# Preparing quantised weights on four engines: VectorE's rounding passes move to ScalarE, scales to GpSimd, context clipping to ScalarE, and the inverse transform ahead of a weight chunk

## The chip, the cores and the metric

The kernel runs on one core of one Trainium2 chip. The metric is the device time of one execution in microseconds (us). Three executions of the kernel before took 1344.51, 1345.06 and 1346.99 us; the median is 1345.06 us.

## The reference, cut to what matters

A two-layer decoder over 2 x 256 tokens of width 512. Layer 0 is an autocorrelation block, an 8-bit product of the tokens with a context, and a feed-forward block with block-quantised weights. Layer 1 is attention over a cache, attention over the context, and a mixture of eight experts. The part that the change touches is in layer 0:

```python
def _quant_elem(x, mbits):           # mbits = 1 for weights
    e = jnp.maximum(jnp.floor(jnp.log2(jnp.maximum(jnp.abs(x), 2.0 ** (-30)))), 0.0)
    step = jnp.exp2(e - mbits)
    return jnp.clip(jnp.round(x / step) * step, -max_norm, max_norm)
def _mx_quant(x, mbits):             # blocks of 32 along the last dimension
    scale = jnp.exp2(jnp.floor(jnp.log2(amax)) - EMAX)
    return (_quant_elem(xb / scale, mbits) * scale).reshape(s)
...
q = jnp.clip(jnp.round(ctx / s + z), 0, 255)      # context, 8 bits
...
corr = irfft(f * conj(f)); weights, delay = top_k(corr, 6)   # autocorrelation taps
x = x + sum_k softmax(weights)[k] * roll(x, delay[k])
```

## The kernel before, in words

Every engine runs a program of its own, written out by hand: it executes its instructions in order, and waits on named semaphores. Nothing reorders them, so the order of the code on an engine is the order of its work.

While VectorE, GpSimd and ScalarE do layer 0's small blocks, the feed-forward weights are brought in as 15 chunks, 11 of 128x1024 (gate and up) and 4 of 128x1408 (down), numbered c = 0 to 14 (`CHUNKS`). SyncE loads chunk c into one of two buffers (`WX`, `load_chunk`). VectorE finds the largest magnitude of each block of 32 (line 916), makes a power-of-two scale and its reciprocal from it (918, 919, 921 or 923), multiplies the chunk by the reciprocal, takes each element's exponent by a mask (936 or 961), makes the rounding constant from it (939 or 962), adds it (940 or 963), subtracts it (943 or 965), clips to +-6 (944 or 966), and multiplies the scale back (945). TensorE then transposes the chunk (`weight_step`, L1325), and ScalarE copies it out of PSUM (L630, L636). For chunks 0 to 5 VectorE does all of it (`weight_chunk`). From chunk 6 on (`SHARED`) GpSimd does the two products with the scales (`normalised`, L521, and `scaled`, L528).

Among the chunks stand other jobs. VectorE finds each row's six taps after chunk 2 (L1005 to L1018), and finishes the taps' softmax after chunk 3 (L1022 to L1024), for which ScalarE computes an exponential (L661). GpSimd fetches the tapped rows by 20 indirect DMAs (L513), and quantises the context, which arrives in four pieces through one buffer `CN` (L502, L505, L507; SyncE loads the next piece once the third of these is done, semaphore `cn_used`). TensorE projects the context for the later attention in 16 steps (`context_step`, L1304 for keys, L1307 for values), two behind each chunk of the table `CONTEXT_AT`; ScalarE copies each step out of PSUM (L624), and there are two PSUM banks for them. The inverse transform (L1345 to L1347) and the weighted sum of the taps (`taps`, L1356, placed by `TAPS_AT`) are TensorE's too. After the last chunk VectorE adds the taps' result to the tokens (L1035), and the second layer norm follows. The rest, attention above all, comes after it.

## Time and profile before

| | |
|---|---|
| Median of three runs | 1345.06 us |
| The profiled execution: its time, its span | 1347.69 us, 1345.8 us |
| Busy over the span: TensorE, VectorE | 1163.9 us (86%), 901.7 us (67%) |
| Busy over the span: ScalarE, GpSimd | 555.8 us (41%), 538.7 us (40%) |
| Weight stage on VectorE | from 23.25 us to 184.45 us |
| VectorE busy from 23.20 to 184.50 us | 152.0 us of 161.3 |

An engine with a large busy share bounds the program only where the others wait for it. So the averages over the whole span say little here: the stage before 184.45 us and the attention after 237 us are bounded by different engines. Instruction rows give the start and the duration; brackets behind a row give the idle time ahead of it and who ended it. PE is TensorE, DVE is VectorE, ACT is ScalarE, POOL is GpSimd, SPq is SyncE's DMA queue.

### The profile page before, as it was taken

The page shows a single profiled execution, that of the slowest core. Times are in us where ns is not written, and L with a number is a line of the kernel's source. Part 1 is how long each engine was busy: PE and PEld are TensorE (multiplying, and loading weights), DVE is VectorE, ACT ScalarE, POOL GpSimd, SP SyncE. Part 2 cuts the span into 40 slices and gives each one's busy share as a digit, 9 for nine tenths or more (in the row PEclk, how much of TensorE's full clock was granted, in tenths as well). Part 3 has the DMA queues.
Part 4 walks back from the last instruction along what each step waited for, and adds up shares of the span by engine and source line. Part 5 has one row for each costly group of instructions (what it writes and reads, how often), then busy time and mean ns, then how long its engine had stood idle before and what let it go on. Part 6 is the DMA issues. An engine that isn't in the chain of part 4 may idle for free.

```text
span 1345.8 us, 16908 instructions
## 1 busy us (share of the span) xinstructions
PE 1163.9 (86%) x5655; PEld 880.9 (65%) x5660; DVE 901.7 (67%) x1432; ACT 555.8 (41%) x1094; POOL 538.7 (40%) x372
## 2 busy tenths in 40 slices
PE   4939624759899999999999999879899999987999
PEld 2413311336688888888888887745678788875787
DVE  6999998886486868686868686554354545543543
ACT  1211222222565656565656565522454535442111
POOL 3774520010464646464645454410454545441000
PEclk9968955879999999999999999989799999999899
DMA  7172442001101010101010101230001010001122
GB/s 289 63 234 91 151 173 74 20 32 40 44 17 59 17 58 16 58 16 58 16 58 16 51 0 55 56 121 24 7 12 37 12 29 0 1 24 63 46 95 78
DMA packets 38834, 77.70 MB, mean 58 GB/s; under 512 B 11395, under 2 KB 19588, under 8 KB 35588
## 3 DMA queue, kind: packets, MB, share of 16 engines
q1 hardware_dynamic: 37188, 71.86, 16.4%
q0 software_dynamic: 1600, 5.24, 1.2%
q8 instruction: 27, 0.44, 0.1%
q14 instruction: 19, 0.16, 0.0%
HBM read 69.75 MB, written 9.44 MB: 59 GB/s over the span
## 4 chain that ended last, share of the span: by engine, by line
PE 71%; DVE 18%; issue 5%; ACT 3%; DMA 1%; POOL 1%; SPq 1%; POOLq 0%; DVEq 0%; ACTq 0%
PE PS L1441 15%; PE PS L1439 15%; PE PS L1440 15%; PE PS L1505 9%; PE PS L1479 5%; DVE nmax L1114 2%; PE PS L1356 2%; PE PS L1407 1%; PE PS L1610 1%; DVE blkamax L916 1%; PE PS L1304 1%; DMA cs<-in_freqs 1%; PE PS L1579 1%; PE PS L1307 1%; DVE PTL L1162 1%
## 5 line engine op out<-in xcount | busy, mean ns | idle before, releaser
L555 POOL TENSOR_TENSOR arena<-arena,rsum 128x768 f32<-128x768 f32 x192 | 281.8, 1468 | 471.5 <-DVE rsum L1119 471.5
L1114 DVE TENSOR_REDUCE nmax<-PS 128x1 f32<-128x768 f32 x192 | 183.5, 956 | 215.8 <-PE PS L1441 213.9
L739 ACT ACTIVATE arena<-PS,nmax 128x768 f32<-128x768 f32 x192 | 173.3, 903 | 252.9 <-DVE nmax L1114 252.8
L1505 PE MATMUL PS<-identf,arena 128*128 128x128 f32 x1152 | 161.1, 276 | 27.7 <-DVE PTL L1162 15.1
L1505 PEld LDWEIGHTS PS<-identf,arena 128*128 128x128 f32 x1152 | 135.6, 141 | 63.8 <-issue 38.8
L1162 DVE TENSOR_TENSOR PTL<-PS,PTH 128x384 fp32r<-128x384 f32 x256 | 129.6, 547 | 1.7 <-ACT PTH L755 1.1
L755 ACT ACTIVATE PTH<-PS 128x384 fp32r<-128x384 f32 x256 | 111.7, 488 | 40.0 <-PE PS L1505 37.7
L1479 PE MATMUL PS<-arena 128*96 128x256 f32 x384 | 87.9, 380 | 0.0
L542 POOL TENSOR_TENSOR WQL<-arena,WQH 128x512 fp32r<-128x512 f32 (+1 forms) x48 | 58.5, 1220 | 60.9 <-ACT WQH L615 60.9
L1439 PE MATMUL PS<-WOH,OTH 128*128 128x512 f32 (+1 forms) x192 | 75.8, 395 | 4.1 <-DVE OTL L1135 3.0
L1439 PE MATMUL PS<-HTH,WQH 128*128 128x512 f32 (+1 forms) x192 | 77.0, 401 | 0.0
L1441 PE MATMUL PS<-WOH,OTL 128*128 128x512 f32 (+1 forms) x192 | 76.3, 397 | 0.0
L1440 PE MATMUL PS<-HTL,WQH 128*128 128x512 f32 (+1 forms) x192 | 76.3, 397 | 0.0
L1441 PE MATMUL PS<-HTH,WQL 128*128 128x512 f32 (+1 forms) x192 | 76.1, 396 | 0.0
L1440 PE MATMUL PS<-WOL,OTH 128*128 128x512 f32 (+1 forms) x192 | 75.7, 394 | 0.0
L1441 PE MATMUL PS<-PTH,VSL 128*128 128x512 f32 x192 | 75.6, 394 | 0.0
L1440 PE MATMUL PS<-PTL,VSH 128*128 128x512 f32 x192 | 75.5, 393 | 0.0
L1129 DVE TENSOR_TENSOR QTL<-arena,QTH 128x512 fp32r<-128x512 f32 (+1 forms) x40 | 67.7, 1694 | 10.6 <-ACT QTH L731 10.6
L1439 PE MATMUL PS<-PTH,VSH 128*128 128x512 f32 x192 | 74.7, 389 | 0.0
L1479 PEld LDWEIGHTS PS<-arena 128*96 128x96 f32 x384 | 61.7, 164 | 17.7
L542 POOL TENSOR_TENSOR WOL<-arena,WOH 128x512 fp32r<-128x512 f32 (+1 forms) x48 | 70.7, 1474 | 0.0
L1119 DVE RECIPROCAL rsum<-psum_exp 128x1 f32<-128x1 f32 x192 | 31.5, 164 | 52.5 <-ACT arena L739 38.7
(243 smaller groups left out, 2528.6 us busy)
## 6 DMA issues: line engine op xcount, KB each, us to landing
arena<-in_wq SPq DMA_DIRECT2D x32, 256.0 KB, 2.6
arena<-in_wo SPq DMA_DIRECT2D x8, 1024.0 KB, 4.8
arena<-in_expert_w SPq DMA_DIRECT2D x8, 1024.0 KB, 4.8
arena<-in_wgu SPq DMA_DIRECT2D x11, 512.0 KB, 3.7
arena<-v_dram SPq DMA_DIRECT2D x8, 384.0 KB, 3.5
arena<-in_wq SPq DMA_DIRECT2D x16, 192.0 KB, 2.8
arena<-in_wo SPq DMA_DIRECT2D x4, 768.0 KB, 5.9
arena<-in_wd SPq DMA_DIRECT2D x4, 704.0 KB, 4.0
```

Of the source, the lines that this page charges most:

```text
L542: pool.tensor_tensor(fr(lo), raw, hi, ALU.subtract).then_inc(s["w_ready"], 1)
L555: pool.tensor_tensor(PR[:, u % 4, :], PR[:, u % 4, :], rsum[:, u % 4:u % 4 + 1].broadcast_to([P, KEYS]), ALU.mult).then_inc(s["pn_ready"], 1)
L739: act.activation(PR[:, slot, :], SC[pair][:, 0:KEYS], ACT.Exp, bias=nmax[:, slot:slot + 1], accum_out=psum_exp[:, slot:slot + 1]).then_inc ...
L755: act.activation(fr(PTH[:, (u // 4) % 2, 3 * half:3 * half + 3, u % 4 * P:(u % 4 + 1) * P]), bank(B_PT[half])[:, 0:3 * P].rearrange("p (k ...
L1114: dve.tensor_reduce(nmax[:, slot:slot + 1], SC[pair][:, 0:KEYS], AX.X, ALU.max, negate=True)\
L1129: dve.tensor_tensor(fr(QTL[0:hd, j, :]), QT[0:hd, j, :], QTH[0:hd, j, :], ALU.subtract)\
L1162: dve.tensor_tensor(fr(PTL[:, (u // 4) % 2, ks, cols]), bank(B_PT[half])[:, 0:3 * P].rearrange("p (k c) -> p k c", k=3), PTH[:, (u // 4) % ...
L1439: pe.matmul(out, fr(xh), fr(yh), start=start, stop=False)
L1440: pe.matmul(out, fr(xh), fr(yl), start=False, stop=False)
L1441: return pe.matmul(out, fr(xl), fr(yh), start=False, stop=stop)
L1479: mm = pe.matmul(bank(B_OT)[0:hd, b * S:(b + 1) * S], VS2[:, b, k, :], PT[:, j % 2, k, b * S:(b + 1) * S], start=k == 0, stop=k == KK - 1)
L1505: mm = pe.transpose(bank(B_PT[half])[:, k * P:(k + 1) * P], PR[:, u % 4, c * P:(c + 1) * P], identf[:])
```

## The change

On VectorE a chunk is now two halves, `weight_normalised(c)` (maxima, scales, product with the reciprocal, exponent mask) and `weight_rounded(c)` (two fused operations, clip), and the order is a pipeline: normalised(c + 1) stands ahead of rounded(c). The rounding constant `max(m, 1) * ROUND/2` becomes a ScalarE activation `magic(c)`, Relu(ROUND/2 * m - ROUND/2), in bf16; the missing ROUND/2 is added inside the two `scalar_tensor_tensor` operations. GpSimd does the product with the scale for all 15 chunks, and no product with the reciprocal. In the context's quantisation the clip moves from GpSimd to three ScalarE activations, and GpSimd's last operation takes its constants from SBUF (`qconst`) instead of from the instruction. GpSimd's 20 gathers no longer stand together but in fours ahead of `scaled(3)` to `scaled(7)`. On TensorE the inverse transform stands ahead of weight chunk 1, the context steps 2 to 7 one chunk later, and the taps behind chunks 9 to 12. SyncE loads chunks 6 and 7 ahead of the second half of the transposed context.

```diff
-        SHARED = 6
-        CONTEXT_AT = {0: (0, 1), 1: (2, 3), 2: (4, 5), 3: (6, 7), 5: (8, 9), 6: (10, 11), 7: (12, 13), 8: (14, 15)}
-        TAPS_AT = {5: 0, 6: 1, 8: 2, 9: 3}
+        CONTEXT_AT = {0: (0, 1), 2: (2, 3), 3: (4, 5), 4: (6, 7), 5: (8, 9), 6: (10, 11), 7: (12, 13), 8: (14, 15)}
+        TAPS_AT = {9: 0, 10: 1, 11: 2, 12: 3}
...
-            load_chunk(5)
+            for c in range(5, 8):
+                load_chunk(c)
             sp.wait_ge(s["ectx_psum"], 8)
             sp.dma_start(CTXT, ctx_t[1].rearrange("(k p) t -> p k t", p=P)).then_inc(s["ctxt_in"], 16)
-            for c in range(6, len(CHUNKS)):
+            for c in range(8, len(CHUNKS)):
...
+            def context_quantised(n):
                 pool.wait_ge(s["ctxn_in"], 16 * (n + 1))
                 pool.tensor_scalar(CN, CN, inv_s[:, 1:2], qs[:, 3:4], ALU.mult, ALU.add)\
+                    .then_inc(s["cn_scaled"], 1)
+                pool.wait_ge(s["cn_clipped"], n + 1)
+                pool.tensor_scalar(CQ[:, n // 2, (n % 2) * 2:(n % 2) * 2 + 2, :], CN, qconst[:, 0:1], qconst[:, 1:2],
+                                   ALU.mult, ALU.add).then_inc(s["cn_used"], 1)
...
+            context_quantised(0)
+            context_quantised(1)
+            for c in range(3):
                 scaled(c)
+                if c < 2:
+                    context_quantised(c + 2)
...
+            for c in range(3, len(CHUNKS)):
+                for n in range(4 * (c - 3), min(4 * (c - 2), RT * LAGS)):
+                    gather(n)
+                scaled(c)
...
+            def magic(c):
+                act.wait_ge(s["wexp_ready"], c + 1)
+                if c >= 2:
+                    act.wait_ge(s["wq_rounded"], c - 1)
+                act.activation(weight_magic(c), WM[:, 0:CHUNKS[c]], ACT.Relu, bias=neg_magic[:, 0:1],
+                               scale=ROUND / 2).then_inc(s["magic_ready"], 1)
...
+            for c in range(len(CHUNKS)):
+                if c + 2 < len(CHUNKS) and c != 2:
+                    magic(c + 2)
+                for w in [c] if c < NCH else [2 * c - NCH, 2 * c - NCH + 1]:
+                    weight_step(w)
+                for n in CONTEXT_AT.get(c, ()):
+                    context_step(n)
+                if c < 2:
+                    context_clipped(c + 2)
+                if c + 1 in TAPS_AT:
+                    tap_diagonals(TAPS_AT[c + 1])
+                if c == 2:
                     act.wait_ge(s["tap_diff"], 1)
                     act.activation(tapw[:], tapv[:], ACT.Exp).then_inc(s["tap_exp"], 1)
+                    magic(c + 2)
...
+            def weight_normalised(c):
...
+                block_scale(w, n, 0.25, blkinvs[c % 3], blkscales[c % 3])
+                dve.tensor_tensor(blocks(nn, n), blocks(w, n), spread(blkinvs[c % 3], n // MX), ALU.mult)\
+                   .then_inc(s["wx_used"], 1)
+                dve.wait_ge(s["wx_used"], c + 1)
+                if c:
+                    dve.wait_ge(s["magic_ready"], c)
+                dve.tensor_scalar(WM[:, 0:n].bitcast(U32), nn.bitcast(U32), EXPONENT, None, ALU.bitwise_and)\
+                   .then_inc(s["wexp_ready"], 1)
+            def weight_rounded(c):
...
+                dve.wait_ge(s["magic_ready"], c + 1)
+                step(dve.scalar_tensor_tensor(nn, mm, ROUND / 2, nn, ALU.add, ALU.subtract))
                 if c >= 2:
                     dve.wait_ge(s["wt_psum"], c - 1 if c - 2 < NCH else NCH + 2 * (c - 2 - NCH) + 2)
+                step(dve.scalar_tensor_tensor(q, mm, ROUND / 2, nn, ALU.add, ALU.subtract))
                 dve.tensor_scalar(q, q, 6.0, -6.0, ALU.min, ALU.max).then_inc(s["wq_rounded"], 1)
...
+            weight_normalised(3)
+            weight_rounded(2)
...
+            weight_normalised(4)
+            weight_rounded(3)
             dve.wait_ge(s["tap_exp"], 1)
```

VectorE, one chunk in the middle of the stage before: the five passes of a 128x1024 chunk, then the next chunk's block maxima and scales (`arena` is the large work area in which most buffers lie, `HT` the second buffer for the normalised chunk).

```order
L961 TENSOR_SCALAR arena<-HT 128x1024
L962 TENSOR_SCALAR arena<-arena 128x1024
L963 TENSOR_TENSOR HT<-HT,arena 128x1024
L965 TENSOR_TENSOR arena<-HT,arena 128x1024
L966 TENSOR_SCALAR arena<-arena 128x1024
L916 TENSOR_REDUCE blkamax<-arena 128x32
L918 TENSOR_SCALAR blkamax<-blkamax 128x32
L919 TENSOR_SCALAR blkscale<-blkamax 128x32
```

The same engine and place now: maxima and scales, product and mask of one chunk, then the three passes of the chunk ahead of it.

```order
L952 TENSOR_REDUCE blkamax<-arena 128x32
L954 TENSOR_SCALAR blkamax<-blkamax 128x32
L955 TENSOR_SCALAR blkscale<-blkamax 128x32
L956 RECIPROCAL blkinv<-blkscale 128x32
L966 TENSOR_TENSOR arena<-arena,blkinv 128x1024
L971 TENSOR_SCALAR arena<-arena 128x1024
L979 SCALAR_TENSOR_TENSOR arena<-arena 128x1024
L982 SCALAR_TENSOR_TENSOR arena<-arena 128x1024
L983 TENSOR_SCALAR arena<-arena 128x1024
```

The pass L962 has left VectorE, and the product L966 has come back to it.

ScalarE before, from the copy of context step 0 to the exponential of the taps (L661), which stands behind context steps 4 and 5 (128x384).

```order
L624 ACTIVATE arena<-PS 96x512 x2
L630 ACTIVATE arena<-PS 128x4x256
L624 ACTIVATE arena<-PS 96x512 x2
L630 ACTIVATE arena<-PS 128x4x256
L624 ACTIVATE arena<-PS 128x384 x2
L661 ACTIVATE tapw<-tapv 128x24
```

ScalarE now, from the clip of context piece 2 (L673 to L677) to the exponential (L701).

```order
L673 ACTIVATE arena<-arena,qconst 128x1024
L675 ACTIVATE arena<-arena,qconst 128x1024
L677 ACTIVATE arena<-arena,qconst 128x1024
L666 ACTIVATE arena<-arena,neg_magic 128x1024
L638 ACTIVATE arena<-PS 128x4x256
L673 ACTIVATE arena<-arena,qconst 128x1024
L675 ACTIVATE arena<-arena,qconst 128x1024
L677 ACTIVATE arena<-arena,qconst 128x1024
L638 ACTIVATE arena<-PS 128x4x256
L632 ACTIVATE arena<-PS 96x512 x2
L701 ACTIVATE tapw<-tapv 128x24
L666 ACTIVATE arena<-arena,neg_magic 128x1024 x2
```

Two clips of the context and the copies of the weight chunks 1 and 2 and of the context steps 2 and 3 now stand between the copy of context step 1 and the exponential.

## Rows read from the trace of the kernel before

**Rows 1.** Busy time by stage, with TensorE's granted clock, DMA share and GB/s

```profile
23.20:67.80 44.60, 42.11 (x127) 19.56 (x125) 42.56 (x73) 8.48 (x13) 28.46 (x10) 1.00 0.27 93
67.80:96.00 28.20, 8.99 (x35) 5.41 (x36) 26.41 (x37) 3.25 (x5) 22.01 (x19) 0.62 0.74 239
96.00:184.50 88.50, 56.84 (x192) 27.58 (x190) 83.03 (x82) 21.26 (x44) 42.16 (x19) 0.81 0.37 120
```

**Rows 2.** Timeline of VectorE, the first half of the stage (start, duration)

```profile
23.25 1.22 DVE L916 TENSOR_REDUCE blkamax<-arena 128x32 f32<-128x1024 f32 x1
...
44.20 1.29 DVE L999 TENSOR_TENSOR arena<-arena 128x512 f32<-128x512 f32 x2
...
56.46 0.42 DVE L1005 COPY arena<-PS 128x256 f32<-128x256 f32 x1
...
67.79 1.21 DVE L916 TENSOR_REDUCE blkamax<-arena 128x32 f32<-128x1024 f32 x1
...
71.12 0.69 DVE L936 TENSOR_SCALAR arena<-arena 128x1024 uint32<-128x1024 uint32 x1
...
72.69 1.23 DVE L940 TENSOR_TENSOR arena<-arena 128x1024 f32<-128x1024 f32 x1
...
75.67 1.23 DVE L945 TENSOR_TENSOR arena<-arena,blkscale 128x1024 bf16<-128x1024 bf16 x1
...
77.33 1.21 DVE L916 TENSOR_REDUCE blkamax<-arena 128x32 f32<-128x1024 f32 x1
```

**Rows 3.** Timeline of VectorE, a 128x1408 chunk and the stage's end

```profile
165.45 1.61 DVE L916 TENSOR_REDUCE blkamax<-arena 128x44 f32<-128x1408 f32 x1
167.10 1.12 DVE L918 TENSOR_SCALAR blkamax<-blkamax 128x44 uint32<-128x44 uint32 x1
...
168.82 0.83 DVE L961 TENSOR_SCALAR arena<-HT 128x1408 uint32<-128x1408 uint32 x1
169.68 3.12 DVE L962 TENSOR_SCALAR arena<-arena 128x1408 f32<-128x1408 f32 x1
...
184.45 2.47 DVE L1035 TENSOR_TENSOR X<-X,PS 128x512 f32<-128x512 f32 x4
```

**Rows 4.** Timeline of VectorE, a fused operation in the feed-forward block

```profile
240.34 1.62 DVE L1080 SCALAR_TENSOR_TENSOR arena<-arena,PS 128x1408 f32<-128x1408 f32 x1
```

**Rows 5.** Timeline of GpSimd: context piece 2 and 3, gathers, a product with scales

```profile
50.40 3.96 POOL L507 TENSOR_SCALAR arena<-arena 128x1024 bf16<-128x1024 f32 x1
58.15 1.20 POOL L502 TENSOR_SCALAR arena<-arena,inv_s,qs 128x1024 f32<-128x1024 f32 x1 [3.79 <-DMA arena<-in_ctx]
...
68.50 1.23 POOL L513 DMA_INDIRECT arena<-h,tapoff  x1 [1.72 <-DVE tapoff L1014]
...
96.78 0.95 POOL L513 DMA_INDIRECT arena<-h,tapoff  x1 [0.30 <-issue]
...
106.69 1.91 POOL L528 TENSOR_TENSOR arena<-arena,blkscale 128x1024 bf16<-128x1024 bf16 x1 [3.61 <-DVE arena L966]
```

**Rows 6.** Groups of instructions on ScalarE up to 236 us (busy, mean ns)

```profile
L610 ACT ACTIVATE H<-X,neg_mean 128x512 f32<-128x512 f32 x12 | 7.7, 710 | 15.0 <-DVE neg_mean L879 15.0
L700 ACT ACTIVATE KCH<-arena 128x1024 fp32r<-128x1024 f32 x4 | 3.9, 1046 | 0.0
```

**Rows 7.** Timeline of TensorE: pairs of context steps, a sum of taps

```profile
38.48 7.06 PE L1304 MATMUL PS<-arena 128*96 128x512 f32 x16
...
77.78 7.26 PE L1307 MATMUL PS<-arena 128*128 128x384 f32 x16
...
132.38 5.38 PE L1307 MATMUL PS<-arena 128*128 128x384 f32 x16
...
141.07 4.56 PE L1356 MATMUL PS<-arena 128*128 128x512 f32 x10 [2.86 <-ACT arena L650]
```

**Rows 8.** Timeline of SyncE's DMA queue behind the taps

```profile
162.25 24.04 SPq L381 DMA_DIRECT2D arena<-in_kcache  x16
...
212.63 1.77 SPq L398 DMA_DIRECT2D arena<-in_wq  x4
```

More of the change, by code:

```diff
@@ L482, in _ @@
             pool.memset(minus_half[:], -0.5).then_inc(s["consts"], 1)
+            pool.memset(neg_magic[:], -ROUND / 2).then_inc(s["consts"], 1)
+            for i, v in enumerate((1.0, -128.0, ROUND, ROUND + 255.0, 255.0)):
+                pool.memset(qconst[:, i:i + 1], v).then_inc(s["consts"], 1)
             pool.wait_ge(s["pool_chain"], 2)
@@ L651, in tap_diagonals, with context_clipped @@
                        .then_inc(s["dg_ready"], 1)
-            squared(0)
-            transposed(0)
+            def magic(c):
+                act.wait_ge(s["wexp_ready"], c + 1)
+                if c >= 2:
+                    act.wait_ge(s["wq_rounded"], c - 1)
+                act.activation(weight_magic(c), WM[:, 0:CHUNKS[c]], ACT.Relu, bias=neg_magic[:, 0:1],
+                               scale=ROUND / 2).then_inc(s["magic_ready"], 1)
+            squared(0)
+            def context_clipped(n):
+                act.wait_ge(s["cn_scaled"], n + 1)
+                act.activation(CN, CN, ACT.Identity, bias=qconst[:, 2:3]).then_inc(s["act_chain"], 1)
+                act.wait_ge(s["act_chain"], 2 * n + 1)
+                act.activation(CN, CN, ACT.Relu, bias=qconst[:, 3:4], scale=-1.0).then_inc(s["act_chain"], 1)
+                act.wait_ge(s["act_chain"], 2 * n + 2)
+                act.activation(CN, CN, ACT.Relu, bias=qconst[:, 4:5], scale=-1.0).then_inc(s["cn_clipped"], 1)
+            transposed(0)
+            act.wait_ge(s["consts"], 8)
+            context_clipped(0)
+            magic(0)
+            magic(1)
+            context_clipped(1)
             for m in range(KT):
@@ L910, in transposed, with block_scale @@
                            .then_inc(s["ht_lo"], 1)
[L912 removed]
+            def block_scale(src, n, down, blkinv=blkinv, blkscale=blkscale):
                 nb = n // MX
@@ L940, in weight_chunk @@
-                step(dve.tensor_tensor(nn, nn, mm, ALU.add))
+                if c >= 3:
+                    dve.wait_ge(s["wq8_ready"], c - 2)
+                block_scale(w, n, 0.25, blkinvs[c % 3], blkscales[c % 3])
[4 more added lines that the diff above has]
+                    dve.wait_ge(s["magic_ready"], c)
@@ L956, in chunk_rounded @@
-            def chunk_rounded(c):
-                n = CHUNKS[c]
-                nn, mm, q = (WN, WN2)[c % 2][:, 0:n], WM[:, 0:n], WQ8[:, c % 2, 0:n]
-                dve.wait_ge(s["wn_ready"], c - SHARED + 1)
-                step(dve.tensor_scalar(mm.bitcast(U32), nn.bitcast(U32), EXPONENT, None, ALU.bitwise_and))
-                step(dve.tensor_scalar(mm, mm, 1.0, ROUND / 2, ALU.max, ALU.mult))
-                step(dve.tensor_tensor(nn, nn, mm, ALU.add))
-                dve.wait_ge(s["wt_psum"], c - 1 if c - 2 < NCH else NCH + 2 * (c - 2 - NCH) + 2)
-                step(dve.tensor_tensor(q, nn, mm, ALU.subtract))
+                step(dve.scalar_tensor_tensor(q, mm, ROUND / 2, nn, ALU.add, ALU.subtract))
@@ L1025, in _ @@
                .then_inc(s["tapw_ready"], 1)
-            for c in range(4, SHARED):
-                weight_chunk(c)
-            chunk_scales(SHARED)
-            for c in range(SHARED, len(CHUNKS)):
+            for c in range(4, len(CHUNKS)):
                 if c + 1 < len(CHUNKS):
-                    chunk_scales(c + 1)
-                chunk_rounded(c)
+                    weight_normalised(c + 1)
+                weight_rounded(c)
             for r in range(RT):
@@ L1347, in _ @@
                 pe.matmul(o, SQ[0:1, 2, rows], nyq_sb[0:1, :], start=False, stop=True).then_inc(s["corr_psum"], 1)
-            for n in CONTEXT_AT[1]:
-                context_step(n)
+            weight_step(1)
             def taps(r):
```

95 lines of the change are left out of this document (27 added, 68 removed).

## The prediction, made before the changed kernel was run

> **What bounds the kernel now.** I read the busy times by stage first. In the weight stage VectorE is busy for 42.56 of 44.60 us, 26.41 of 28.20 and 83.03 of 88.50, ScalarE for a fifth at most [rows 1]. So up to 184.45 us, where the taps are added, VectorE's own passes set the time; the other engines matter only where they make it wait. Next the timeline of VectorE gives marks: A 23.25 (first chunk), B 67.79 (taps found, chunk 3 begins), C 77.33 (softmax of the taps done, chunk 4 begins), D 184.45 [rows 2, 3]. What follows D keeps its order and its work; it moves as a block if D moves. I count at D alone.
>
> One pass costs more than its elements. The rounding constant L962 takes 3.12 us for 1408 elements, the mask L961 of the same size 0.83; and L918 takes 1.12 us for 44 elements [rows 3]. Each stands where GpSimd is at work on a product with scales: VectorE's single-source passes wait for it, its maxima (1.61 before L918) do not.
>
> **VectorE's new work.** For 128x1024, maxima, scales, product and mask run from 67.79 to 71.12 + 0.69: 4.05 with the gap. Add, subtract and clip run from 72.69 to 75.67 [rows 2]: 2.98; I take 2.9, as two fused operations take their place and no pass waits behind the clip. The trace has no fused operation on two SBUF tensors, one in bf16. The nearest takes 1.62 us for 1408 elements [rows 4], 1.15 ns each, the rate of the 1.23 us for 1024 of L940 [rows 2]; I take that, 1.26 with its gap. The lower end is the same; the upper is a fused operation at two passes' price, 2.5. So a chunk costs 6.95 where it cost 9.0 (77.33 - 67.79 = 9.54, of which 0.5 is the taps' softmax). For 1408: 168.82 - 165.45 = 3.37, less 0.93 of waiting, plus product 1.66 and mask 0.87, with gaps 5.05; rounding 2 x 1.66 + 0.5 = 3.8 [rows 3, 4].
>
> To B: 4 first halves 16.2, 3 second halves 8.7, the power sum 1.2, the taps' search 67.79 - 56.46 = 11.3, and 0.8 of waits behind GpSimd [rows 2]: 23.25 + 38.2 = 61.4, against 67.79.
>
> From C to D: 6 x 4.05 + 4 x 5.05 + 7 x 2.9 + 4 x 3.8 = 80.0. On top come the waits behind `scaled`, which now starts as each chunk's clip ends, just when VectorE begins a maximum. A product of 1.91 [rows 5] outlasts 1.25 by 0.66 (five times), a 1408 maximum by 0.3 (twice), and the long product costs 0.93 (twice): 5.8. In chunks 5 to 7 GpSimd has four gathers too, at (96.78 - 68.50)/19 = 1.49 us each [rows 5]: 5.9 + 1.9 = 7.8 a chunk, against VectorE's 7.6. The product then starts some 0.3 late, three times. Together 7 us, so C to D is 87.0, against 107.1.
>
> **The new wait, at C.** The exponential of the taps' softmax stands behind a long queue on ScalarE. I follow it. The context's first product takes 1.20; GpSimd's last takes 3.96 now with constants in the instruction, and its new form has them in SBUF, as the 1.20 one has [rows 5]. I take 1.2 and keep 3.96 for the range. A ScalarE pass over 1024 elements takes 1.05, and the one with a bias operand, 0.71 for 512, bounds it from above at 1.4 [rows 6]; I take 1.16, so three in a chain are 3.5. Piece 1 is asked for at 27.1, behind the load of chunk 2 that waits for chunk 0's product (23.25 + 3.3); piece 3 took 3.8 to land [rows 5], this one shares the DMA engines with a chunk and gets 4.8: 31.9, 33.2 scaled, 36.8 clipped, 38.0 stored. `scaled(0)` 40.0, transposes and context steps 0 and 1, 7.06 [rows 7]: 47.6. ScalarE copies, then clips piece 2 to 51.7; stored 53.0. Piece 3 needs 3.8 from there to land [rows 5], and 1.2 + 3.5 + 1.2: 62.6. `scaled(2)` 64.5. Context steps 2 and 3: 0.6 + 7.0, and TensorE has idled for 9 us by then. After the idle stretch from 67.80 to 96.00 with its granted clock of 0.62 [rows 1] a pair of value steps took 7.26, at full clock 5.38 [rows 7]; I add 2.1: 74.1. Copy and exponential: 74.9. VectorE would be at the softmax at 61.4 + 6.95 + 1.6 (behind `scaled(2)`) = 69.9, so it stands for 5 us. C comes at 75.5, against 77.33. The same 5 us hide anything lost before B.
>
> D = 75.5 + 87.0 = 162.5, which is **21.9 us earlier**.
>
> **What I cost at nothing.** `magic(c)`, 1.1 us (1.5 for the long chunks), is hidden: it stands behind the copy and two context steps of chunk c - 3, done at least 6 us before VectorE's next mask. In chunks 5 and 6, each with two key steps of 3.5 and a second context tensor that SyncE asks for only at 90.2 by this count, TensorE finishes about when `magic(8)` and `magic(9)` are due; no wait in my count, but 6 us of slack for `magic(9)` at most. Taps: chunk 12 is transposed at 152.7, the sum takes 5.4 [rows 7], ends 158.0; VectorE needs it at 162.5. SyncE's 16 key loads come behind it, 24.04 us, to about 186 with the issue; the load of wq that follows now waits to 212.63, which is D + 28.2 [rows 8], and would be due at 190.7. So 4 us of slack there. GpSimd's six small memsets lie in its idle start.
>
> Against the profiled execution, 1347.69, this gives 1325.8. That execution is 2.6 above the median; from the median, 1345.06 - 21.9 = **1323.2**.
>
> A rule speaks against the change. ScalarE idles in the stage: 21.26 of 88.50 us busy [rows 1], and passes of 1.16 on it are not on the path. The Trainium skill (ScalarE: Activation LUTs, Rules for kernel authors) says to use VectorE, not ScalarE, for Relu, add and multiply. By that rule the constant would stay on VectorE, 11 x 0.72 + 4 x 0.87 = 11.4 us, and the time would be 1334.6. The trace speaks for the engine that is free.
>
> **The rivals.**
> - GpSimd's last context pass stays slow. For it: its output is bf16, as that of the 3.96 row [rows 5]. Against: the only visible difference of the 1.20 row is where its constants lie, besides that type. It delays the exponential to 85.4, and D to 173.0: 1333.7.
> - TensorE holds up ScalarE, hence the constants. The clock was 0.62 and 0.81 in this stage [rows 1], and I assume it full from 75 us on. For full: a chunk's key pair and transposes fill 7.6 us, a value pair 5.9; a key pair after 38 us took 7.06 at clock 1.00 [rows 1, 7]. If each step from 2 on took 1.5 times as long, VectorE would wait 3.2 and 2.3 us for constants: D 169.8, 1330.4. At twice (half clock throughout) the exponential comes at 79.7, then masks 9 to 12 wait 6.0, 6.6, 2.8 and 4.9, and D is 188.3: **1348.9, slower than before**. It crosses at 1.9 times.
> - The taps are late: at half clock each sum takes 10.6, the last ends at 169.4: D 169.5, 1330.1.
> - The change doesn't do what it says: the fused operations are slower than the passes they replace. At 1.8 each for 1024, D is 175.4, 1336.0; at 2.1 nothing is gained; at 2.5, 1357. Against: rows 4's rate.
> - It is better than I count: no idle-clock penalty and products that VectorE doesn't feel give D 153.4: 1314.0. Against: L918's 1.12 [rows 3].
>
> **How the numbers follow.** A difference under 0.2% (2.7 us) can hardly be told from none here. Chances: forecast, within 1316 to 1329, 0.66; slow context pass 0.10; TensorE late in part (1.2 to 1.8 times, or the taps) 0.10; fused operations somewhat slow 0.05; better than 1316, 0.03; about no change 0.02; slower, by the clock 0.02, by the fused operations 0.02. The range 1315 to 1336 holds the forecast and most of the next three. Faster 0.94, same 0.02, slower 0.04.
>
> **What would show it.** Maxima of the 1024 chunks 7.6 to 7.9 us apart on VectorE, where chunk 3 took 9.0; fused operations at 1.23 and 1.62; an idle stretch of about 5 us ahead of the tap sum's reduction, ended by ScalarE's exponential; the small L918-like operation still at 0.8 to 1.2; ScalarE's clips at 1.1 to 1.2; D near 162.5. Wrong would be idle time ahead of the mask or the fused operations, ended by ScalarE, or ahead of D's addition, ended by TensorE.

## The result: 1327.2 us, 18.8 less than before

The changed kernel's four executions took 1326.07 to 1328.56 us, median 1327.2; four of the kernel before on the same chip took 1344.51 to 1349.08, median 1346.03. The ratio is 0.9858, with a 95% interval of 0.9836 to 0.988. The forecast was 1323.2, with a range of 1315 to 1336. Five more executions later gave a median of 1327.43, so the comparisons below are made with 1327.3.

The marks in the profiled execution (1326.17 us, span 1324.3):

| mark | before | predicted | after |
|---|---|---|---|
| A, first chunk | 23.25 | 23.25 | 22.40 |
| B, taps found | 67.79 | 61.4 | 64.39 |
| C, softmax of the taps done | 77.33 | 75.5 | 78.88 |
| D, the taps' addition | 184.45 | 162.5 | 169.90 |
| from D to the end of the span | 1161.35 | the same | 1154.4 |

So the total is right by two errors that happen to cancel: D came 7.4 us later than predicted, and the part behind D, which was to move as a block, was 7.0 us shorter. That they cancel is luck; with the first alone the sum would have come to 1330.6. Of the 14.55 us gained at D, 0.85 are there at A already: a small VectorE operation just ahead of it, which took 1.01 beside GpSimd's slow pass over the context, takes 0.17 now.

Busy time by stage of the changed kernel, to be read as [rows 1] (span of the window; then PE, PEld, DVE, ACT and POOL busy; PEclk, DMA share, GB/s). VectorE still sets the stages before B and behind C, but with 7.0 idle us behind C; between B and C it idles for 5.7 of 14.5. An operation that is held up by another engine while it runs counts as busy here.

```profile
22.40:64.40 42.00, 31.08 (x88) 14.06 (x86) 40.49 (x72) 20.56 (x22) 14.00 (x8) 0.93 0.34 120
64.40:78.90 14.50, 11.18 (x36) 5.12 (x37) 8.78 (x14) 3.00 (x6) 12.41 (x10) 0.72 0.43 134
78.90:169.90 91.00, 69.10 (x231) 33.88 (x229) 83.98 (x94) 36.69 (x60) 36.75 (x23) 0.88 0.44 146
```

Its timeline of VectorE, the places where it stood or was slow, and two that ran as predicted (start, duration; in brackets idle time and who ended it):

```profile
32.19 2.11 DVE L982 SCALAR_TENSOR_TENSOR arena<-arena 128x1024 bf16<-128x1024 bf16 x1
...
39.51 2.92 DVE L979 SCALAR_TENSOR_TENSOR arena<-arena 128x1024 f32<-128x1024 bf16 x1
...
65.86 1.84 DVE L955 TENSOR_SCALAR arena<-blkamax 128x32 f32<-128x32 f32 x1
...
78.35 0.18 DVE L1044 TENSOR_REDUCE tapm<-tapw 128x4 f32<-128x24 f32 x1 [5.41 <-issue]
...
82.81 1.22 DVE L979 SCALAR_TENSOR_TENSOR arena<-arena 128x1024 f32<-128x1024 bf16 x1
...
94.38 1.19 DVE L954 TENSOR_SCALAR blkamax<-blkamax 128x32 uint32<-128x32 uint32 x1
...
105.55 1.22 DVE L952 TENSOR_REDUCE blkamax<-arena 128x32 f32<-128x1024 f32 x1 [4.53 <-DMA arena<-in_wgu]
...
163.91 1.62 DVE L979 SCALAR_TENSOR_TENSOR arena<-arena 128x1408 f32<-128x1408 bf16 x1
165.56 3.86 DVE L982 SCALAR_TENSOR_TENSOR arena<-arena 128x1408 bf16<-128x1408 bf16 x1
...
169.90 2.47 DVE L1054 TENSOR_TENSOR X<-X,PS 128x512 f32<-128x512 f32 x4
```

A fused operation takes 1.22 or 1.62 where nothing is in its way, as forecast. Two waits stand out: 5.41 us ahead of L1044, for which this trace names no releaser (three others, with the same wait, name ScalarE's exponential), and 4.53 us ahead of chunk 8's maxima. GpSimd's timeline, same kernel, shows the other side of the slow passes:

```profile
31.44 1.79 POOL L513 TENSOR_SCALAR arena<-arena,inv_s,qs 128x1024 f32<-128x1024 f32 x1 [6.97 <-DMA arena<-in_ctx]
36.88 2.16 POOL L516 TENSOR_SCALAR arena<-arena,qconst 128x1024 bf16<-128x1024 f32 x1 [3.65 <-ACT arena L677]
39.01 2.34 POOL L530 TENSOR_TENSOR arena<-arena,blkscale 128x1024 bf16<-128x1024 bf16 x1
...
54.74 1.20 POOL L516 TENSOR_SCALAR arena<-arena,qconst 128x1024 bf16<-128x1024 f32 x1 [9.98 <-ACT arena L677]
...
164.07 3.87 POOL L530 TENSOR_TENSOR arena<-arena 128x1408 bf16<-128x1408 bf16 x1 [7.14 <-DVE arena L983]
```

Read the two together at the end. L979 ends at 165.5; GpSimd's product, called at 164.07, takes 2.56 from there (165.5 + 2.56 = 168.1), and shows 3.87. L982, called at 165.56, takes its 1.62 from the end of that product and shows 3.86. By these times each waits for the whole of the other.

ScalarE's and TensorE's timelines show why L1044 stood: the exponential L701 ended at 78.3 (74.9 predicted), behind the context steps 2 and 3, which TensorE worked on from 68.55.

```profile
53.49 1.15 ACT L677 ACTIVATE arena<-arena,qconst 128x1024 f32<-128x1024 f32 x1
...
78.11 0.21 ACT L701 ACTIVATE tapw<-tapv 128x24 f32<-128x24 f32 x1
```

```profile
41.92 8.69 PE L1323 MATMUL PS<-arena 128*96 128x512 f32 x16
...
67.72 1.03 PE L1344 MATMUL PS<-identb,arena 128*128 128x128 bf16 x8 [9.24 <-POOL arena L530]
68.55 9.03 PE L1323 MATMUL PS<-arena 128*96 128x512 f32 x16
```

SyncE's DMA queue, where chunk 8's load stands behind that of the context's second half (which waits for context step 7):

```profile
96.20 0.38 SPq L372 DMA_DIRECT2D arena<-in_ctx_t  x1
96.63 12.63 SPq L346 DMA_DIRECT2D arena<-in_wgu  x3
```

### The profile page after: what moved, and what is told of

Read it like the earlier page. It is cut to its first block, busy times and chain, and to the rows that moved or that the text cites. A ratio compares the mean times of both kernels' runs of the same rounds, so it can differ in the third digit from the quotient of the medians.

```text
span 1324.3 us, 16950 instructions
## 1 busy us (share of the span) xinstructions
PE 1160.2 (88%) x5655; PEld 877.6 (66%) x5660; DVE 882.2 (67%) x1420; ACT 586.1 (44%) x1121; POOL 504.7 (38%) x371
## 4 chain that ended last, share of the span: by engine, by line
PE 68%; DVE 20%; issue 6%; ACT 2%; DMA 2%; POOL 1%; SPq 1%; POOLq 0%; DVEq 0%; ACTq 0%
PE PS L1457 16%; PE PS L1458 16%; PE PS L1459 15%; PE PS L1523 9%; PE PS L1497 5%; DVE nmax L1133 2%; DVE blkamax L952 2%; DVE arena L982 2%; DVE arena L979 1%; PE PS L1628 1%; DVE arena L966 1%; DMA cs<-in_freqs 1%; PE PS L1597 1%; DVE PTL L1181 1%; PE PS L1307 1%
## 5 line engine op out<-in xcount | busy, mean ns | idle before, releaser
L1523 PE MATMUL PS<-identf,arena 128*128 128x128 f32 x1152 | 159.5, 274 | 27.9 <-DVE PTL L1181 15.4
```

Of the source, the lines that this page charges most:

```text
L1523: mm = pe.transpose(bank(B_PT[half])[:, k * P:(k + 1) * P], PR[:, u % 4, c * P:(c + 1) * P], identf[:])
```

## The experiments

All are edits of the changed kernel, unless stated; times are medians of 4 to 5 executions (12 for the last). Medians of the same kernel differ by 2 to 3 us between batches, so smaller differences are read from the marks of the trace alone. The marks vary too: in traces of kernels with the same order ahead of chunk 8, the wait for it took 4.53 to 5.02 us, and D of the changed kernel itself differs by 0.6.

| run | C | D | time | ratio to before, 95% |
|---|---|---|---|---|
| changed kernel | 78.88 | 169.90 | 1327.2 | 0.9858 (0.9836 to 0.9880) |
| changed kernel, again | 78.97 | 170.49 | 1327.43 | 0.9848 (0.9833 to 0.9863) |
| chunk 8 first | 79.2 | 167.78 | 1326.24 | 0.9842 (0.9819 to 0.9864) |
| exponential early | 75.24 | 162.98 | 1321.18 | 0.9810 (0.9787 to 0.9833) |
| constant on VectorE | 79.12 | 174.29 | 1333.93 | 0.9903 (0.9880 to 0.9926) |
| clip on GpSimd | 82.09 | 173.72 | 1330.40 | 0.9868 (0.9843 to 0.9893) |
| inverse transform late | 83.48 | 172.21 | 1329.25 | 0.9870 (0.9852 to 0.9888) |
| additions sooner | 79.05 | moved | 1325.80 | 0.9842 (0.9826 to 0.9858) |
| three moves | 75.14 | moved | 1320.46 | 0.9806 (0.9790 to 0.9822) |
| GpSimd's last constants in the instruction | 78.40 | 169.81 | 1324.42 | 0.9827 (0.9808 to 0.9846) |
| scale on VectorE | 76.40 | 170.77 | 1327.29 | 0.9854 (0.9838 to 0.9871) |
| three moves and those constants | 75.38 | moved | 1320.33 | 0.9795 (0.9779 to 0.9810) |
| kernel before, again | | 184.27 | 1349.38 | 1.0012 (0.9998 to 1.0025) |

### Chunk 8's load ahead of the context's second half

```diff
-            for c in range(5, 8):
+            for c in range(5, 9):
                 load_chunk(c)
             sp.wait_ge(s["ectx_psum"], 8)
             sp.dma_start(CTXT, ctx_t[1].rearrange("(k p) t -> p k t", p=P)).then_inc(s["ctxt_in"], 16)
-            for c in range(8, len(CHUNKS)):
+            for c in range(9, len(CHUNKS)):
```

> Changed kernel with one thing moved on SyncE's queue: the load of weight chunk 8 stands ahead of the second transposed context instead of behind it. Theory: VectorE's 4.5 us of idle time ahead of chunk 8's maxima came only from that order (the load was issued at 96.63, behind a wait for context step 7, and landed after 1 MB of context). Then the idle time is gone, and the taps' addition, mark D, comes at 165.4 instead of 169.90; the whole 4 to 5 us faster than the changed kernel. Rival: the context steps 8 and 9 start later by as much, ScalarE's constants for chunks 8 and 9 become late, and VectorE waits for those: D at 168 or later.

The wait of 4.53 us is gone, so its cause is shown. But D gained only 2.12 of it, and came (167.78) just below where the rival had it. VectorE now ran ahead of the others: the mask of a later chunk stood 0.93 us for ScalarE's constant, as the rival said, and the small operations behind a maximum lost 1.3 us more to GpSimd's product; C was 0.3 later. VectorE's timeline of this run:

```profile
102.47 1.18 DVE L954 TENSOR_SCALAR blkamax<-blkamax 128x32 uint32<-128x32 uint32 x1
...
114.23 0.69 DVE L971 TENSOR_SCALAR arena<-arena 128x1024 uint32<-128x1024 uint32 x1 [0.93 <-ACT arena L666]
```

### The exponential ahead of the copy of chunk 2

```diff
             for c in range(len(CHUNKS)):
                 if c + 2 < len(CHUNKS) and c != 2:
                     magic(c + 2)
+                if c == 2:
+                    act.wait_ge(s["tap_diff"], 1)
+                    act.activation(tapw[:], tapv[:], ACT.Exp).then_inc(s["tap_exp"], 1)
                 for w in [c] if c < NCH else [2 * c - NCH, 2 * c - NCH + 1]:
                     weight_step(w)
+                if c == 2:
+                    magic(c + 2)
                 for n in CONTEXT_AT.get(c, ()):
                     context_step(n)
```

(and the same three lines are taken out behind the context steps.)

> Changed kernel with ScalarE's order changed in one place: the exponential of the taps' softmax stands ahead of the copy of weight chunk 2, and the rounding constant of chunk 4 ahead of the copies of context steps 2 and 3. Theory: the 5.4 us that VectorE stood still at mark C were this exponential's place in the queue; C comes at 73.5 instead of 78.88, and D 5.4 to 7.3 us earlier (the wait for chunk 8's load shrinks too): 162.6 to 164.5. Rival: the wait only moves to the next thing that comes from that chain, the constants or the transposes of chunks 2 to 4, and D stays above 168.

The theory held but for C: the reduction behind the exponential began at 72.88 with no idle time ahead of it, D came at 162.98, 6.92 earlier, and the time fell by 6.1. C came at 75.24, not at 73.5, since a small softmax operation now waits for GpSimd's product (2.02 us); and 0.78 us are left of the wait for chunk 8. It is the one edit whose gain is clear of the spread between batches.

```profile
73.30 2.02 DVE L1047 TENSOR_TENSOR tapw<-tapw,tapm 128x24 f32<-128x24 f32 x1
...
98.20 1.22 DVE L953 TENSOR_REDUCE blkamax<-arena 128x32 f32<-128x1024 f32 x1 [0.78 <-DMA arena<-in_wgu]
...
162.98 2.47 DVE L1055 TENSOR_TENSOR X<-X,PS 128x512 f32<-128x512 f32 x4
```

### The rounding constant back on VectorE

```diff
+                dve.tensor_scalar(weight_magic(c), WM[:, 0:n], 1.0, ROUND / 2, ALU.max, ALU.mult)\
+                   .then_inc(s["magic_ready"], 1)
...
-                step(dve.scalar_tensor_tensor(nn, mm, ROUND / 2, nn, ALU.add, ALU.subtract))
+                step(dve.scalar_tensor_tensor(nn, mm, 0.0, nn, ALU.add, ALU.add))
```

(the second fused operation likewise, the waits ahead of the pass are not shown, and ScalarE's `magic` is left out.)

> Changed kernel with the rounding constant back on VectorE, as one single-source pass with bf16 output (0.7 to 0.9 us for each of the 15 chunks, 11.4 us in all); ScalarE has no part in it. Theory: VectorE bounds the stage except at its waits (5.4 us at C, 4.5 at chunk 8), which swallow what is added ahead of them: of 11.4 us some 2.9 before C and 2.2 before chunk 8 are absorbed, so D at about 176 (6 us later). Rival A: VectorE is not the bound, D stays within 1 us of 169.90. Rival B: the pass pays for GpSimd as well, with every gather and product that it meets, and costs 15 us or more.

The time rose by 6.6 us and D by 4.39; 2.0 more lie in a stretch of attention far behind D, which is looked at in the last experiment. The passes themselves took 8.5 us for eleven and 3.6 for four, 12.1 together. The waits at C (5.41 us, now none) and for chunk 8 (4.53, now 0.84) took most of that off, since VectorE reached those places later. D came 1.7 below the theory's 176; both rivals fell. The prediction had put this version 11.4 us above its forecast: it had the passes about right, and took nothing off for the waits that absorb them.

The Trainium skill (ScalarE: Activation LUTs, Rules for kernel authors) would keep multiply and maximum on VectorE. Followed here, that rule costs 4.4 us at D: VectorE's pass over 128x1024 is the shorter one (0.69 us against ScalarE's 1.15), but it lies on the path, and ScalarE's does not.

### The clip of the context on GpSimd again

```diff
+                pool.tensor_scalar(CN, CN, qconst[:, 0:1], qconst[:, 1:2], ALU.max, ALU.min)\
+                    .then_inc(s["cn_clipped"], 1)
...
-                pool.tensor_scalar(CQ[:, n // 2, (n % 2) * 2:(n % 2) * 2 + 2, :], CN, qconst[:, 0:1], qconst[:, 1:2],
-                                   ALU.mult, ALU.add).then_inc(s["cn_used"], 1)
+                pool.tensor_scalar(CQ[:, n // 2, (n % 2) * 2:(n % 2) * 2 + 2, :], CN, qconst[:, 2:3], qconst[:, 3:4],
+                                   ALU.add, ALU.add).then_inc(s["cn_used"], 1)
```

with 0, 255 and the two rounding constants in `qconst`, and ScalarE's clips left out.

> Changed kernel with the context's clip and rounding back on GpSimd in three passes as before the change, but all constants read from SBUF instead of from the instruction; ScalarE has no clip. Theory: what made two of these passes cost 3.6 to 4.0 us was where their constants were, so each takes 1.2 to 1.3 us, a piece takes 3.7 instead of 5.9, the exponential no longer comes late, C at about 73.5 and D 5 to 7 us earlier than 169.90. Rival: maximum and minimum are slow on GpSimd in themselves (3.6 us): a piece takes 6.1, C and D stay within 1.5 us.

GpSimd's timeline of this run:

```profile
18.39 3.78 POOL L516 TENSOR_SCALAR arena<-arena,qconst 128x1024 f32<-128x1024 f32 x1
22.27 3.83 POOL L518 TENSOR_SCALAR arena<-arena,qconst 128x1024 bf16<-128x1024 f32 x1
...
59.76 1.20 POOL L513 TENSOR_SCALAR arena<-arena,inv_s,qs 128x1024 f32<-128x1024 f32 x1 [1.61 <-DMA arena<-in_ctx]
```

All three have their constants in SBUF. The (max, min) and the (add, add) pass take 3.8 us, the (multiply, add) pass 1.20; before the change the two slow ones, with their constants in the instruction, took 3.63 to 3.96. So the theory fell, and the rival's reason held for both slow pairs. D rose by 3.8, more than the rival's 1.5, because it had counted (add, add) as fast. This is also what the clip on ScalarE is worth at D.

### The same pass with its constants in the instruction

```diff
-                pool.tensor_scalar(CQ[:, n // 2, (n % 2) * 2:(n % 2) * 2 + 2, :], CN, qconst[:, 0:1], qconst[:, 1:2],
+                pool.tensor_scalar(CQ[:, n // 2, (n % 2) * 2:(n % 2) * 2 + 2, :], CN, 1.0, -128.0,
                                    ALU.mult, ALU.add).then_inc(s["cn_used"], 1)
```

> The changed kernel, with the constants of GpSimd's last pass over the context (multiply, add) in the instruction instead of in SBUF. Theory, after the run with GpSimd's clip (max and min, add and add with constants in SBUF took 3.8 us): the pair of operations sets the price and the place of the constants does not, so the pass still takes 1.20 and nothing moves: D 169.9, time 1326 to 1328.5. Rival, the prediction's reason (constants in the instruction make it slow): the pass takes 3.9, the exponential comes 5 to 8 us later, D about 173 to 177, time 1331 to 1335.

```profile
23.29 1.05 POOL L516 TENSOR_SCALAR arena<-arena 128x1024 bf16<-128x1024 f32 x1 [4.98 <-ACT arena L677]
```

GpSimd's pass takes 1.05 us, less than the 1.20 with constants in SBUF. With the run above this settles it for these three pairs: the pair of operations decides between 1.1 and 3.8 us, not where the constants lie. D did not move (169.81). The median was 2.9 us lower than the changed kernel's, and this is not explained. For spread between batches speak the profiled executions (1325.95 here, 1326.17 there) and the run with all four edits, which gained nothing over three; against it speaks the changed kernel run again, which by this reading was expected at 1324.5 to 1326 and came at 1327.43.

### The inverse transform behind the transposes of chunk 1

```diff
+            weight_step(1)
             pe.wait_ge(s["power_ready"], 2)
             for r in range(RT):
...
-            weight_step(1)
```

> The changed kernel with one thing put back: TensorE's inverse transform stands behind the transposes of weight chunk 1 again. Those wait for GpSimd's product with chunk 1's scales, which ends at 57.8 us in the changed kernel's trace, so the first correlation row is there at about 60.2 instead of 52.9 and mark B moves from 64.39 to 71.6. Theory (as the prediction says, the wait of 5.4 us for the exponential at C hides whatever is lost before B, since ScalarE's queue sets C): the wait ahead of the tap sum shrinks from 5.41 to about 0, C and D move by 0 to 1.5 us, time 1327 to 1329. Rival (the earlier inverse transform is what the gain rests on, or the gathers, asked for 7 us later, hold up the products of chunks 5 to 7): D moves by 5 to 7 us, time 1332 to 1334.

VectorE stood 8.65 us for the correlations, and once more for each row (0.60 to 0.67), B came at 74.40, 10.0 us later than in the changed kernel (7.2 expected). TensorE had idled for 7.26 us ahead of chunk 1's transposes and took 1.06 to 1.23 us for each pair of matmuls behind them, where the changed kernel has 0.60 to 0.70; that made the first row later than counted, and VectorE wait for the others, 1.9 us together. At C nothing was left to wait for: the reduction at 81.44 follows its clip directly. The next maxima began at 83.48, 4.6 later, and the wait for chunk 8 fell from 4.53 to 2.22, so that D lost 2.31 and the time 1.9. Neither range held the value: D came between them, nearer to the theory's.

```profile
61.65 0.43 DVE L1026 COPY arena<-PS 128x256 f32<-128x256 f32 x1 [8.65 <-PE PS L1366]
...
81.44 0.17 DVE L1044 TENSOR_REDUCE tapm<-tapw 128x4 f32<-128x24 f32 x1
```

So the sooner inverse transform, moved to gain at B, is worth 2.3 us at D and not 10. The rest lies in the shadow of the waits for the exponential and for chunk 8.

### The taps' additions ahead of the last chunk's rounding

```diff
                 if c + 1 < len(CHUNKS):
                     weight_normalised(c + 1)
+                else:
+                    for r in range(RT):
+                        dve.wait_ge(s["tap_psum"], r + 1)
+                        dve.tensor_tensor(X[:, r, :], X[:, r, :], bank(r), ALU.add).then_inc(s["tap_added"], 1)
                 weight_rounded(c)
-            for r in range(RT):
-                dve.wait_ge(s["tap_psum"], r + 1)
-                dve.tensor_tensor(X[:, r, :], X[:, r, :], bank(r), ALU.add).then_inc(s["tap_added"], 1)
```

> The changed kernel, with VectorE's four additions of the taps' result put ahead of the two fused operations and the clip of the last chunk. The second of these fused operations took 3.86 us (1.62 elsewhere) while GpSimd's product with chunk 13's scales ran. Theory (VectorE's operations with two inputs in SBUF wait for GpSimd's product, and one with an input in PSUM does not): the additions take 2.47 for the four beside the product of 2.56, the fused operations take 1.62 each, and the layer norm's first reduction begins at 170.2 instead of 172.41: time 1324.8 to 1326, 1.2 to 2.4 lower. Rival (any VectorE operation waits, PSUM or not): the additions take 4.7 to 5, the reduction stays at 172.4, time 1327.2.

VectorE's and GpSimd's timelines of this run:

```profile
164.54 2.47 DVE L1054 TENSOR_TENSOR X<-X,PS 128x512 f32<-128x512 f32 x4
166.93 1.81 DVE L979 SCALAR_TENSOR_TENSOR arena<-arena 128x1408 f32<-128x1408 bf16 x1
168.78 1.62 DVE L982 SCALAR_TENSOR_TENSOR arena<-arena 128x1408 bf16<-128x1408 bf16 x1
...
170.88 2.46 DVE L911 TENSOR_REDUCE arena<-X 128x64 f32<-128x512 f32 x4
...
176.84 1.28 DVE L920 TENSOR_REDUCE arena<-H 128x64 f32<-128x512 f32 x2 [2.56 <-ACT H L618]
```

```profile
164.71 2.56 POOL L530 TENSOR_TENSOR arena<-arena 128x1408 bf16<-128x1408 bf16 x1 [7.14 <-DVE arena L983]
```

On the lock the theory held: additions with one operand in PSUM took 2.47 beside a product that took its 2.56, and the fused operations 1.81 and 1.62 instead of 1.62 and 3.86. The Trainium skill (SBUF — State Buffer, SBUF: two separate sides) says that a VectorE operation with two SBUF inputs and a GpSimd operation that reads SBUF lock each other out for a whole instruction; these rows agree. Not every pass of GpSimd does so: in the run with the clip on GpSimd, VectorE's product L964 with two SBUF inputs, begun at 49.09 in the middle of a (max, min) pass (47.23 to 51.02), took 1.23 us, and that pass its 3.79. On the time it failed. The layer norm's first reduction began 1.5 earlier (170.88), but the next, L920, waits for ScalarE, whose copy of the last chunk's transposes stands ahead of it in its queue, and came at 176.84 where the changed kernel has 176.61. The median, 1.5 us lower, lies in the theory's range, but not for the theory's reason.

### Three moves, and four

> Three moves together: chunk 8's load ahead of the context's second half (as e1), the exponential ahead of the copies of chunk 2 (as e2), and the additions ahead of the last chunk's rounding (as e6). Theory (the waits are separate): e2's D 162.98 less what is left of the wait for chunk 8 (0.8) and less 2.2 at the end; layer norm's first reduction at 162.5 to 163.2 where e2 had 165.48, time 1318 to 1319. Rival (with the loads earlier, VectorE runs ahead of ScalarE and GpSimd and waits for them instead, as in e1, where 2.1 of 4.5 us were gained): 1320 to 1321.5.

> The three moves of e7 and the constants of GpSimd's last context pass in the instruction, where it took 1.05 us instead of 1.20. Theory: the second context pass ends 0.15 sooner in the chain to the exponential, D 0 to 0.4 lower than e7, time 1319.5 to 1320.5. Rival (the 2.8 us between the run with these constants, 1324.42, and the changed kernel's first runs, 1327.2, are this edit's and not the spread between batches): time 1317 to 1318.5.

These are the edits of chunk 8's load, the exponential and the additions together, then with GpSimd's constants in the instruction too. The first reduction began at 163.22 and 163.51, but the second at 169.19 and 169.47, against 169.69 with the exponential alone. So the moves added at most 0.5 us to that one edit, and the medians (1320.46, 1320.33, 1321.18) don't tell them apart. The theory for three moves (1318 to 1319) fell, for the reason of the run before, and the time lay in the rival's range; with GpSimd's constants in the instruction too, the time lay where the theory had it, but the first reduction 0.3 later and not sooner, so nothing was won, and the rival, that this edit is worth 2.8 us, fell. The best version measured is some 7 us faster than the changed kernel, nearly all by the exponential.

### The product with the scale back on VectorE

```diff
                 dve.tensor_scalar(q, q, 6.0, -6.0, ALU.min, ALU.max).then_inc(s["wq_rounded"], 1)
+                dve.wait_ge(s["wq_rounded"], c + 1)
+                dve.tensor_tensor(blocks(q, n), blocks(q, n), spread(blkscales[c % 3], n // MX), ALU.mult)\
+                   .then_inc(s["wq8_ready"], 1)
```

(and GpSimd's `scaled` is left out.)

> The changed kernel, with the product with the scale back on VectorE behind each clip, for all 15 chunks; GpSimd keeps only the context passes and the gathers. It prices what GpSimd's product is worth once VectorE's waits behind it are counted. Theory: from C on VectorE gets seven products of 1.26 and four of 1.66 more, 15.5 us, and loses the waits behind GpSimd's product (about 6 by the prediction, 2.2 more at the stage's end) and 3 of the 4.5 us for chunk 8, which it now reaches later. No single-source pass and no fused operation takes longer than alone (0.18, 0.69, 1.23, 1.62), chunks are 8.2 to 8.3 us apart, D comes at 175 to 178, time 1332 to 1335. Rival (the waits cost about what the product does, so the move to GpSimd bought nothing): D 169 to 172, time 1326.5 to 1329.

My theory fell and the rival held: D 170.77 against 169.90, the time equal (1327.29). Busy time by stage:

```profile
22.40:67.60 45.20, 38.52 (x111) 17.15 (x109) 43.57 (x75) 22.50 (x25) 9.39 (x7) 0.93 0.32 110
67.60:76.40 8.80, 0.38 (x4) 0.38 (x5) 8.46 (x15) 1.37 (x2) 6.59 (x6) 0.64 0.62 192
76.40:170.80 94.40, 71.95 (x240) 35.15 (x237) 91.54 (x106) 36.67 (x60) 18.02 (x15) 0.86 0.44 147
```

VectorE is busy for 91.54 of 94.40 us behind C, with only the gaps between its instructions left. From C to D it takes 94.37 us; the changed kernel takes 91.02, of which 4.53 is the wait for chunk 8, so 86.5. GpSimd's products therefore save 7.9 us of the 15.4 (7 x 1.25 + 4 x 1.66); the other 7.5 are given back as waits behind GpSimd (the lengthened operations of VectorE from C to D add up to 7.7). And what they save is lost twice more. TensorE's transposes no longer wait in GpSimd's queue, the exponential comes at 67.69, and C at 76.40, 2.5 sooner than in the changed kernel. And VectorE reaches chunk 8 when it has landed. 7.9 less 2.5 less 4.5 leaves 0.9. That the move pays once those waits are gone follows from a comparison, and was not tried apart: this version has no wait left to lose, and the changed kernel with the exponential early comes to D 7.8 us sooner (162.98).

### The two kernels again: where 7 us behind D come from

> The changed kernel again, nothing altered, beside the others on one chip. If its first value holds: 1326.5 to 1328, D 169.9, and after D the spacing 110.2 and 104.6 us between the output weights' loads and the next in the second attention, as in every run of it and its variants. If the lower time of the run with GpSimd's constants in the instruction was spread between batches, this one comes out at 1324.5 to 1326 too.

> The kernel before again, nothing altered. Of the 18.8 us that the change gained, only 14.55 lie ahead of D; the trace of before lost 4.8 and 1.8 us in two stretches of the attention over the context, at a granted clock of 0.85 to 0.99 where all variants of the changed kernel show 1.00, and the code there is the same. Theory 1 (it comes with the kernel before, as its later start or what preceded the stage): the new trace shows 115.0 and 106.4 again. Theory 2 (chance in one execution): it shows 110.2 and 104.6, the span is some 6.6 us less than in the first trace, and D is 184.4; then part of the 4 us is to be looked for between runs, not in the change.

In the second attention over the context, the load of the query weights is issued, and that of the output weights follows one group later. SyncE's queue, of the kernel before, of its second trace, and of the changed kernel:

```profile
919.54 90.21 SPq L398 DMA_DIRECT2D arena<-in_wq  x8
1034.53 0.35 SPq L403 DMA_DIRECT2D arena<-in_wo  x1
```

```profile
919.98 89.48 SPq L398 DMA_DIRECT2D arena<-in_wq  x8
1034.24 0.35 SPq L403 DMA_DIRECT2D arena<-in_wo  x1
```

```profile
903.25 85.54 SPq L407 DMA_DIRECT2D arena<-in_wq  x8
1013.43 0.35 SPq L412 DMA_DIRECT2D arena<-in_wo  x1
```

That is 114.99 and 114.26 us before, and 110.18 after; in all twelve traces of the changed kernel and its variants it is 110.18 to 110.20, with D anywhere from 163 to 174. The code is the same. The difference is TensorE's granted clock, in windows of 5 us of the kernel before, its second trace, and the changed kernel's second trace:

```profile
951.00:956.00 5.00, 3.09 (x14) 2.58 (x15) 1.75 (x4) 2.05 (x5) 2.07 (x2) 0.60 0.00 2
956.00:961.00 5.00, 3.39 (x13) 2.84 (x13) 1.58 (x3) 1.86 (x5) 2.42 (x2) 0.50 0.00 0
961.00:966.00 5.00, 5.00 (x18) 4.09 (x18) 1.59 (x3) 1.44 (x4) 2.07 (x2) 0.54 0.01 2
```

```profile
956.00:961.00 5.00, 3.39 (x15) 2.84 (x13) 1.58 (x3) 1.60 (x4) 2.94 (x3) 0.50 0.00 0
961.00:966.00 5.00, 5.00 (x16) 3.66 (x15) 1.59 (x3) 1.48 (x3) 2.03 (x3) 0.50 0.00 2
```

```profile
941.00:946.00 5.00, 3.51 (x20) 2.91 (x21) 2.93 (x5) 2.07 (x4) 3.17 (x4) 1.00 0.00 2
946.00:951.00 5.00, 5.00 (x29) 3.98 (x28) 1.66 (x4) 2.48 (x7) 1.47 (x1) 1.00 0.18 43
```

Before, 10 to 14 us run at the lower clock (1.2 GHz, granted clock 0.50 to 0.60 over 15 us in the first trace, 0.50 over 10 in the second); the changed kernel has the full clock (2.4 GHz) there, after an equally light stretch. The mean granted clock of whole executions agrees: 0.931 to 0.939 in 29 executions of the kernel before, 0.943 to 0.948 in nine of the changed kernel. So the 4.1 to 4.8 us come with the kernel before: my second theory fell for this stretch. It held for the one behind it: 106.36 us against 104.60, but 104.77 in the second trace of before, so these 1.8 us are chance of one execution.

The changed kernel also had 1.7 and 2.5 us less from D to this attention. The clock accounts for that too. The first stretch of its kind, from the load of the output weights to that of the next query weights, took 26.66 us before and 24.65 after, with the same 93 matmuls at a mean granted clock of 0.81 and 0.93:

```profile
291.65:318.31 26.66, 22.55 (x93) 19.38 (x94) 16.57 (x31) 5.91 (x10) 1.01 (x1) 0.81 0.12 40
277.88:302.53 24.65, 20.34 (x93) 17.95 (x94) 16.53 (x31) 5.91 (x10) 1.01 (x1) 0.93 0.13 44
```

This one does not go with the kernel: it took 24.62 to 24.67 us in both traces of the changed kernel and in three variants (three moves, constants in the instruction, scale on VectorE), and 26.55 to 27.02 in the other seven and in both of before. So a variant can be 2 us slower or faster behind D without a cause in its edit. In the experts' part the changed kernel took 1.5 and 0.6 us more; this was not followed up. Why the clock falls in one execution and not in the other is open: no kernel was run with its start alone shifted by some us.

## Why the prediction came out right, step by step

- **The seam of the stage** (D 162.5, was 169.90). The step that failed first is "Copy and exponential: 74.9": it ended at 78.3, so C was 3.4 late. Context steps 0 and 1 began 1.4 late and took 8.69 where I put 7.06: TensorE had idled for 4.32 us ahead of chunk 0's transposes, and its granted clock was 0.63 over the next 4.6 us, 1.00 behind them (I had charged that to the second pair alone, which took 9.03, as counted). ScalarE's clip of piece 2 ended 2.9 later than counted, and all that followed.
- **The wait for chunk 8** (4.53 us) was in no term. I counted SyncE's request for the second context half, at 90.2, as TensorE's problem only and did not follow the queue to the load behind it.
- **VectorE against GpSimd.** I charged the small operations behind a maximum, and got those about right (0.87 to 1.19 for L954). I missed that fused operations with two SBUF inputs wait as well: 2.24 us at the stage's end (L982, 3.86), and 4.4 between 32 and 45 us, where a mask and a clip waited too (L982 0.9, mask 0.9, L979 1.7, clip 0.9). Mostly by these B was 3.0 late, in the shadow of the wait at C. The rest of C to D was 2.8 shorter than my sum (91.02 - 4.53 - 2.24 = 84.25 against 87.0): the other waits behind GpSimd were 5.5 and not 7, and a chunk that met none took 6.79 and not 6.95.
- **Fused operations** took 1.22 and 1.62: exact. The rival that they cost more is refuted.
- **ScalarE's passes** took 1.15 (1.16 forecast). `magic` was hidden, and the taps were in time; the key loads and the wq load too (D + 28.17, 28.2 forecast).
- **GpSimd's last pass** took the 1.20 I chose, for a wrong reason: two runs show that the pair of operations matters, and that constants in the instruction are even faster (1.05).
- **"The same 5 us hide anything lost before B"** is shown: of 10 us lost there, 5.4 were hidden, 4.6 came through to C and, with the wait for chunk 8, 2.3 to D.
- **What follows D moves as a block** failed: in two stretches of attention the clock gave 4.1 to 4.8 and 2.0 to 2.2 us. Without them the result would have been 1333 to 1334, in the range but 10 us from the forecast.
- **TensorE holds up ScalarE, D 169.8**: D fell there, but behind C no mask or fused operation stood for ScalarE. Of that rival's mechanism only the first pair of context steps occurred (8.69 for 7.06), and it acted through the exponential, not the constants.

The gain is thus 14.55 us of the weight stage (13.78 between the second traces) and 6 to 7 of clock in the profiled executions. At D, taking the constant off VectorE is worth 4.4 us, the clip on ScalarE 3.8, the sooner inverse transform 2.3; the product with the scale, the half of the change that uses GpSimd, is worth 0.9 at most by itself as the kernel stands. These do not add up to the whole, since they share the same waits, and the rest was not undone apart: the order of the two halves, the gathers in fours, the later taps and the earlier loads.

## What to carry to other kernels

When an engine is relieved, follow each queue that it will now catch up with, as far as its next waits: some 10 us of VectorE's relief were spent on an exponential behind copies of the context that had nothing to do with it, and on a load behind an unrelated wait. Before giving GpSimd an elementwise product of VectorE's, price what VectorE's two-input passes will wait behind it: here half of the saving. And compare the part of the program that a change does not touch: a sum over the changed part can be wrong, and the total right.

## What the runs showed of the hardware that I had not expected

- GpSimd's pass over 128x1024 with two constants took 1.05 us (multiply, add; constants in the instruction), 1.20 (the same, constants in SBUF) and, where nothing held it up, 3.63 to 3.83 (max, min; add, add), whether the constants lay in SBUF or in the instruction.
- VectorE's fused operation with two SBUF inputs and GpSimd's product wait for each other's whole length (3.86 for 1.62, 3.87 for 2.56); VectorE's addition with a PSUM operand did not wait, nor did it make the product wait. Beside a (max, min) pass of GpSimd a VectorE product with two SBUF inputs ran unhindered (1.23).
- The same stretch of attention ran with 10 us or more at the lower clock in both traces of one kernel (114.3 and 115.0 us for the group), and took 110.2 us in all twelve of the other and its variants. Another took 24.6 us at a mean granted clock of 0.93 in five traces and 26.6 to 27.0 at 0.81 in the rest, with the same instructions.
